# A two-layer graph kernel on one core: 144 layer-1 gathers in another order, with two fills after each four in place of a wait for their landing

## What is computed

```python
h = jnp.maximum(_layernorm(x), 0.0)
# layer 0: scores are taken only where adj > 0
scores = where(adj > 0, h @ W0 @ input.T, NEG_PAD)
x = x + softmax(scores / 0.07, axis=1) @ input
h = jnp.maximum(_layernorm(x), 0.0)
# layer 1
h = h @ W1
e = leaky_relu((h @ a_src)[:, None] + (h @ a_dst)[None, :], 0.2)
att = softmax(where(adj > 0 and h.sum(1) != 0, e, NEG), axis=1)
att = where(att >= THR, att, 0) * (number of valid), 0 where top <= THR
x = x + elu(h + att @ h)
```

## Time and profile before

| | us |
|---|---|
| median of 3 runs | 780.8 |
| lowest and highest | 780.02, 783.97 |
| profiled execution | 790.29 |
| its span, from first to last instruction | 788.7 |
| POOL busy in it | 323.8 (41%) |
| DVE busy | 516.2 (65%) |
| PE busy | 412.1 (52%) |
| ACT busy | 410.0 (52%) |

### The profile page before, as it was taken

How to read it: one execution, slowest core, us unless ns; L and a number is a source line. 1 busy time by engine, 2 the same in 40 slices (tenths; PEclk the granted TensorE clock), 3 DMA queues, 4 the chain that set the end, 5 groups by cost and what they waited for, 6 DMA issues and landing times.

```text
span 788.7 us, 9476 instructions
## 1 busy us (share of the span) xinstructions
PE 412.1 (52%) x2947; PEld 278.3 (35%) x2947; DVE 516.2 (65%) x1921; ACT 410.0 (52%) x424; POOL 323.8 (41%) x352
## 2 busy tenths in 40 slices
PE   3342637676677666676567586655105200154573
PEld 0010314334353434353344354345105100154563
DVE  0029657989898989798778687785154100369895
ACT  4456766778878788878578586613002000012212
POOL 5000221515151525242617364565766555566500
PEclk9566868798988898889779677955655555566777
DMA  8999697999999999999899999222122312123322
GB/s 326 422 420 415 246 329 293 325 360 306 381 313 389 320 392 318 383 310 390 277 334 335 303 345 315 75 58 42 47 49 48 79 40 41 39 54 89 90 95 84
DMA packets 37478, 186.78 MB, mean 237 GB/s; under 512 B 7856, under 2 KB 8112, under 8 KB 18864
## 3 DMA queue, kind: packets, MB, share of 16 engines
q1 hardware_dynamic: 28208, 167.02, 55.6%
q0 software_dynamic: 9216, 19.11, 12.1%
HBM read 179.73 MB, written 6.37 MB: 236 GB/s over the span
## 4 chain that ended last, share of the span: by engine, by line
DVE 34%; DMA 18%; POOL 14%; issue 14%; PE 10%; ACT 8%; another core or an unknown queue 1%; SPq 0%; POOLq 0%; DVEq 0%; ACTq 0%
DMA arena<-in_adj 10%; POOL arena L811 7%; DMA arena<-table,idx_near 6%; ACT arena L861 6%; PE K L1412 4%; DMA E<-table,idx_near 3%; POOL E L811 2%; DVE keys L1017 2%; PE G L1623 2%; DVE s_e L1124 2%; POOL X L790 1%; POOL arena L790 1%; DVE RTp L1182 1%; DVE G L1123 1%
## 5 line engine op out<-in xcount | busy, mean ns | idle before, releaser
L861 ACT ACTIVATE arena<-arena,half_c 128x2048 bf16<-128x2048 int32 x144 | 283.3, 1998 | 70.9 <-DMA arena<-in_adj 52.5
L790 POOL DMA_INDIRECT X<-in_L_gnn_input,idx_all x132 | 129.7, 982 | 305.2 <-DVE idx_near L1096 236.3
L1412 PE MATMUL K<-arena,bits 128*128 128x512 bf16 x576 | 171.4, 439 | 21.7 <-ACT arena L861 20.8
L811 POOL DMA_INDIRECT arena<-table,idx_near x96 | 99.3, 1035 | 70.8 <-DMA arena<-table,idx_near 44.4
L1412 PEld LDWEIGHTS K<-arena,bits 128*128 128x128 bf16 x576 | 59.7, 109 | 94.2 <-ACT arena L861 28.0
L1017 DVE MAX8 keys<-K 128x8 int32<-128x128 f32 x192 | 42.5, 283 | 55.0 <-PE K L1412 55.0
L811 POOL DMA_INDIRECT E<-table,idx_near x48 | 45.3, 943 | 40.2 <-DMA E<-table,idx_near 25.9
L1424 PE MATMUL G<-g,R_all 128*128 128x128 bf16 x324 | 29.5, 250 | 43.4 <-DVE s_e L1124 28.4
L1410 PE MATMUL K<-key_add,key_one 128*128 128x512 bf16 x48 | 21.7, 453 | 54.0 <-DVE keys L1017 30.3
L1424 PEld LDWEIGHTS G<-g,R_all 128*128 128x128 fp8e4 x324 | 24.4, 114 | 53.2 <-issue 32.4
L982 ACT ACTIVATE cand<-cand,zero_c 128x128 f32<-128x128 f32 x6 | 2.4, 402 | 75.2 <-DVE cand L1313 72.2
(11 more groups left out here) (244 smaller groups left out, 1035.8 us busy)
## 6 DMA issues: line engine op xcount, KB each, us to landing
arena<-in_adj SPq DMA_DIRECT2D x144, 1024.0 KB
table<-hs SPq DMA_DIRECT2D x12, 262.0 KB
hs<-table SPq DMA_DIRECT2D x12, 262.0 KB
E<-in_L_gnn_input SPq DMA_DIRECT2D x1, 3072.0 KB, 23.8
out_x<-x_all SPq DMA_DIRECT2D x12, 256.0 KB
x_all<-in_x SPq DMA_DIRECT2D x1, 2560.0 KB, 17.5
X<-in_L_gnn_input,idx_all POOLq DMA_INDIRECT x132
arena<-table,idx_near POOLq DMA_INDIRECT x96, 2.7
```

What stands on the lines that cost most here:

```text
L790: pool.indirect_dma_start(out=x_of(b)[:, e, :], out_offset=None, in_=inp, in_offset=bass.IndirectOffsetOnAxis(ap=idx_all[:, at:at + 1], ax ...
L811: pool.indirect_dma_start(out=E[g][:, t, :], out_offset=None, in_=tables[g], in_offset=bass.IndirectOffsetOnAxis(ap=idx_near[:, t, g:g + 1 ...
L861: nc.scalar.activation(sign[:, load % RING, :], ring[:, load % RING, :], ACT.Sign, bias=half_c[:], scale=1.0).then_inc(signed, 1)
L1412: last = mm(bank_[:], bits[:, third * TB + j, :], sign[:, load % RING, j * FOLD:(j + 1) * FOLD], start=False, stop=(third == G - 1 and j = ...
```

## The change

`mean` is cut in two parts, `scale_mean` (now L801) and `add_mean` (now L807). `records(g, first, last)` takes a range of tiles, and after each fourth gather it calls `pause()`: two chained fills (L814) of `mean_w`, 128x512 float32, with zeros. It no longer waits for the four to land. Each group of four in the stream is held until a given load has been folded, and there are three such groups in each of the steps 8 to 10 and two in step 11. The order after the stream is another one.

```diff
--- before.py
+++ after.py
@@ -792,28 +792,36 @@
                             in_offset=bass.IndirectOffsetOnAxis(ap=idx_all[:, at:at + 1], axis=0)
                         ).then_inc(X_r[b], 16)
 
-                def mean(b):
+                def scale_mean(b):
 
                     if b == 0:
                         pool.wait_ge(mean_kept, 1)
-                    pool.wait_ge(hx_r, b + 1)
                     pool.wait_ge(empty_r, b + 1)
                     size = SIZES[b]
                     link(pool.tensor_tensor(mean_w[:, 0:size], mean_b[:].unsqueeze(1).broadcast_to([P, size, D]),
                                             empty_all[:, tiles(b)].unsqueeze(2).broadcast_to([P, size, D]), ALU.mult))
-                    pool.tensor_tensor(x_all[:, tiles(b), :], x_all[:, tiles(b), :], mean_w[:, 0:size], ALU.add
+
+                def add_mean(b):
+
+                    pool.wait_ge(hx_r, b + 1)
+                    pool.tensor_tensor(x_all[:, tiles(b), :], x_all[:, tiles(b), :], mean_w[:, 0:SIZES[b]], ALU.add
                                        ).then_inc(mean_added, 1)
                     pool.wait_ge(mean_added, b + 1)
 
-                def records(g, i):
-
-                    for t in range(i * Q, (i + 1) * Q):
+                def pause():
+
+                    for _ in range(2):
+                        link(pool.memset(mean_w[:], 0.0))
+
+                def records(g, first, last):
+
+                    for t in range(first, last):
                         pool.indirect_dma_start(
                             out=E[g][:, t, :], out_offset=None, in_=tables[g],
                             in_offset=bass.IndirectOffsetOnAxis(ap=idx_near[:, t, g:g + 1], axis=0)
-                        ).then_inc(E_r[g][i], 16)
+                        ).then_inc(E_r[g][t // Q], 16)
                         if t % FEW == FEW - 1:
-                            pool.wait_ge(E_r[g][i], 16 * (t - i * Q + 1))
+                            pause()
 
                 def third_stored(g):
 
@@ -821,32 +829,36 @@
                         pool.wait_ge(table_stored[q], 16 * len(range(q, last_of(g) + 1, 2)))
 
                 EARLY = 8
-                HALF = BG // 2
                 for n in range(1, NB):
-                    neighbours(n - 1, 0, HALF)
+                    neighbours(n - 1, 0, BG // 2)
                     if n >= 2:
-                        mean(n - 2)
-                    neighbours(n - 1, HALF, BG)
+                        scale_mean(n - 2)
+                        add_mean(n - 2)
+                    neighbours(n - 1, BG // 2, BG)
                     if n == EARLY:
                         pool.wait_ge(inp_summed, 1)
                         third_stored(0)
                     if n >= EARLY:
-                        records(0, n - EARLY)
+                        for k in range(3):
+                            first = 12 * (n - EARLY) + 4 * k
+                            if first + 4 <= FROM[n]:
+                                pool.wait_ge(folded, min((FROM[n] + SIZES[n]) * G + 2 * k + 2, T * G))
+                                records(0, first, first + 4)
                 pool.wait_ge(folded, T * G)
+                scale_mean(NB - 2)
+                add_mean(NB - 2)
                 third_stored(1)
-                records(1, 0)
-                records(1, 1)
-                mean(NB - 2)
-                neighbours(NB - 1, 0, HALF)
-                mean(NB - 1)
-                neighbours(NB - 1, HALF, BG)
-                for i in range(2, NQ):
-                    records(1, i)
-                for i in range(NB - EARLY, NQ):
-                    records(0, i)
+                records(1, 0, 2 * Q)
+                neighbours(NB - 1, 0, BG // 2)
+                scale_mean(NB - 1)
+                add_mean(NB - 1)
+                neighbours(NB - 1, BG // 2, BG)
+                records(1, 2 * Q, 5 * Q)
+                records(0, FROM[NB - 1], T)
                 third_stored(2)
-                for i in range(NQ):
-                    records(2, i)
+                records(2, 0, 2 * Q)
+                records(1, 5 * Q, T)
+                records(2, 2 * Q, T)
 
             @block.scalar
             def _(act):
```

## The result

The changed kernel takes 754.94 us (median of 4 runs, 751.77 to 758.33) against 781.97 for the kernel before (4 runs, 780.02 to 783.97): a ratio of 0.9642 with a 95% interval of 0.9602 to 0.9682, faster. The forecast was 750 us, 740 to 764. The medians fell by 27.0 us, where the sum had 30.6. Ratios and intervals use only the runs in the faster of two states (an execution over 1.5% above its kernel's fastest counts as slow), so that a ratio can differ a little from that of two medians.

The account below looks back on a forecast made before the run. The `adj` stream fills DMA, then POOL's gathers ahead of table 2 bind, later DVE. Terms +5.0 - 0.5 - 3.8 - 40.5 + 9.2 = -30.6 us off the 780.8 median give 750 us, range 740 to 764.

Parts of the forecast that it names:

- The pause: POOL, behind each four gathers: two fills cost 1.4 us in place of a 2.04 us landing wait; group 6.1 us.
- the rival of 762 us: In-flight gathers hold POOL, so a group of four stays at 6.73 us and only the order counts; chance 0.15.
- The stream: Loading of `adj`, steps 8 to 10: twelve more gathers at 0.42 us each cost +5.0 us; ends +10 and -4.
- the gift of -4: Rival in the stream: spacing lets loads pass between groups, -4 us in place of +5, 741 us; chance 0.10.
- the 1.1 us a gather: Rival that the stream pays, steps 8 to 10: from this cost on the change decides for slower; chance 0.10, slower 0.03.
- 0.83 us a gather by the step starts: Higher stream cost, from the starts of steps 7 to 9: 16 gathers cost 13.3 us; used for the +10 end.
- the -0.5 at step 11: Start of step 11: the first neighbour gather no longer waits for a landing and starts with its indices, -0.5 us.
- Step 11 to N: Up to N, the end of batch 11's last neighbour gather: six pauses replace six landing waits, -3.8 us.
- N to `take(0)`: From batch 11's last neighbour gather to `take(0)`: 28 gathers before table 2 instead of 48; 96.5 to 56 us, -40.5.
- `take(0)` to `take(2)`: Two groups of table 1 now stand between table 2's second and third eight gathers: 28.8 to 38 us, +9.2.
- Behind `take(2)`: From `take(2)` to the end: DVE still needs its 84.8 us and POOL's gathers keep up, so 0.
- The rule on fills: Weightings beside POOL: trace row suggests DVE may hold fills, 0.8 us more; the skill says write-only fills never wait.

Follow-up runs that it names:

- the experiment on the late groups: Changed kernel with the last two groups of table 1 behind ten groups of table 2 instead of four; 755.86 us, 0.953 of the kernel before.

## Why the prediction was right, point by point

*The pause* was sized to the hundredth: 592.49 - 590.15 - 0.95 = 1.39 us from the end of a fourth gather to the next, for 1.4. The fills took 0.535 us in the mean, for 0.52. That POOL does not wait for the gathers in flight (the rival of 762 us) is shown by every kernel here, by the one without fills above all: it gives 16 gathers in 20 us. The rival's fear was right in one respect that it didn't name: the density has a price, and whatever waits for PE's results pays it.

*The stream* cost more than the middle and less than the end: +7.7 us from step 7 to 11, for +5.0 - 0.5. In the kernels run beside each other on one chip the same stretch took 172.9 us with 24 gathers (before's order with fills) and 175.5, 175.9 and 178.1 with 36, so +2.6 to +5.2. These are single traces and differ by themselves by some 2 us: the +5 for twelve gathers lies within +2.6 to +7.7 and is shown no closer, and neither the gift of -4 nor the 1.1 us a gather that would have decided for "slower" was seen. The prediction's 0.83 us a gather by the step starts left out step 10, which also had eight: over all three steps it is 0.70 (16.9 us for 24), and twelve at that price are 8.4, nearer to this pair than the 5.0. The term that failed is the -0.5 at step 11: its first neighbour gather came at 505.01, with 8.71 us of "issue" ahead of it. It didn't wait for a landing, but in all likelihood for its batch's indices, which were as late as the stream; in the kernel without fills the same wait, of 8.54 us, names them (DVE idx_near). The step starts are 38.7 us apart for step 7, and 48.4, 45.4 and 45.5 for steps 8 to 10, where 43 to 48 were expected.

*Step 11 to N*: -3.8, as worked out. *N to `take(0)`*: 56.5 us for 56. Table 2's first gather came 43.8 us behind N in place of 43.0, as one gather of the last group was stretched to 1.76. SP read the last records back at 621.71, N + 41.8 for the 41.9 expected, and POOL's pause ended 1.8 us later, so the tables were there in time, though only just. *`take(0)` to `take(2)`*: 38.3 for 38, and the experiment on the late groups shows that it is these two groups: moved, they leave 26.2.

*Behind `take(2)`* the forecast had 0 and the trace -2.9. Before, DVE stood idle twice there with a releaser that the trace doesn't name; the changed kernel has no such row in either of its traces.

DVE in time in the kernel before:

```profile
709.80 0.56 DVE L1306 TENSOR_REDUCE cand<-W 128x128 f32<-128x384 f32 x1 [3.33 <-remote]
...
741.17 0.56 DVE L1306 TENSOR_REDUCE cand<-W 128x128 f32<-128x384 f32 x1 [1.11 <-remote]
```

They stand before the same operation as two of those in the kernel with one fill. The 84.8 us that I took for DVE's own pace thus held 4.4 us of waiting for W, which PE writes. Whether gathers made that wait too is not shown; their pace was slower there.

In this pair of traces the sum came out at -32.0 for -30.6, but 5.4 us of it are in two stretches that the forecast gave nothing (-2.5 before step 7, where the programs are the same, and -2.9 at the end), and 3.2 the other way in the stream. That these nearly cancel is luck. By the medians the gain was 27.0 us, 3.6 less than the sum; no trace stands at the medians, so the stretch that holds these 3.6 us is not known.

*The rule on fills.* The fills lasted 525 ns at the least, 532 in the median and 552 at the most, although pairs of them lay beside a weighting (the one at 597.18 for 1.06 of its 1.13 us), while gathers met by a weighting grew to 2.51 us, as in the kernel before. DVE in time in the changed kernel, two weightings:

```profile
596.48 1.76 DVE L1194 TENSOR_TENSOR RTp<-RT_all,p_e 128x1536 f32<-128x1536 fp8e4 x1
...
680.47 1.76 DVE L1368 TENSOR_TENSOR RTp<-RT_all,above 128x1536 f32<-128x1536 fp8e4 x1
```

And POOL in time, the pair of fills beside the first and the gather beside the second:

```profile
597.18 1.13 POOL L814 MEMSET mean_w<- 128x512 f32 x2
...
680.55 2.51 POOL L819 DMA_INDIRECT arena<-table,idx_near  x1 [0.27 <-POOL mean_w L814]
```

So the 0.8 us that I had weighed for held fills is not there. The Trainium skill (SBUF — State Buffer, section Who interferes with whom) says that a DVE operation with two SBUF inputs does not hold off a GpSimd operation that only writes SBUF. The trace agrees: 0.552 us was the longest of 72 fills.

## What to carry to other kernels

When one engine stands idle for tens of microseconds until another's queue reaches its data, first count what stands in that queue ahead of the data: here the order gave more of the time to the first take than the cheaper pause did, though each gave 2% of the whole. Look then at what the reordering makes late next, and stop where the queue's own total bounds the end. And try a throttle between gathers at several rates before it is taken out: the engine that is throttled gains nothing by it, and yet others may depend on it.

## What was unexpected of the hardware

Gathers of 128 rows issued back to back on POOL (0.94 us each, pitch 1.25 us) delay what needs PE's results by tens of microseconds, with the DMA engines at a share of 0.26 and POOL itself undisturbed. DVE read SB and SA 24.1 and 43.8 us after the end of the rows in which PE wrote them, against 0.03 us for SB in the changed kernel, and later PE itself had one matmul of 0.20 us every 2.80 us. The kernel took 835 us for some 760. At a pitch of 1.39 us it cost the layer-0 tail 4.5 us, at 1.52 nothing, and there gaps of 0.6, 1.4 or 2.6 us did alike.

Why this happens stays open. The ends of matmuls are modelled in the trace, so it does not tell whether the matmuls were done late or only their signals came late. It names no releaser, POOL's instructions are not longer, and no kernel here separated the making of the descriptors, their transfers and the writes of the semaphores.
